# A gated delta-rule attention and mixture-of-experts kernel: the written order of one pipeline slot is replaced, and two more slots stand ahead of its loop

## The reference, cut to what matters

```python
def layer(x):                                  # x: 16 sequences of 512 tokens, 256 channels, f32
    x = x + layernorm(attn(layernorm(x)))
    return x + layernorm(experts(layernorm(x)))

def attn(x):                                   # H = 16 heads, DK = 64, DV = 128
    q, k, v = x @ w_q, x @ w_k, x @ w_v
    beta = 2 * sigmoid(x @ w_b)
    g = -exp(A_log) * softplus(x @ w_a + dt_bias)
    q, k, v = [silu(causal_conv(t, w, taps=4)) for t, w in ((q, conv_q), (k, conv_k), (v, conv_v))]
    q, k = q * rsqrt(sum(q * q) + 1e-6), k * rsqrt(sum(k * k) + 1e-6)     # per head
    for t in range(512):                       # per sequence and head, S is DK x DV
        S = S * exp(g[t])
        S = S + outer(k[t], (v[t] - k[t] @ S) * beta[t])
        o[t] = (q[t] * DK ** -0.5) @ S
    y = o * rsqrt(mean(o * o) + 1e-5) * norm_w * silu(x @ w_g)
    return y @ w_out                           # 2048 channels down to 256
```

## Time and profile before

| what | value |
|---|---|
| time, median of 3 runs | 4893.17 us (4889.53 to 4895.24) |
| the profiled execution: its time, and its span from first to last instruction | 4890.76 us, 4889.5 us |
| PE busy, PEld busy | 98%, 79% of the span |
| DVE, ACT, POOL busy | 86%, 71%, 64% of the span |
| delta phase on PE | first product of slot 0 at 124.66 us, last product at 4553.3 us |
| one ACT copy `b_Ue` or `b_Me`; one product of `c_y` on DVE (two in a step) | 374, 387 ns; 343 ns |
| mean granted TensorE clock | 0.991 of full speed |

### The profile page before, as it was taken

The page is one execution under the profiler, slowest core; times in us unless marked ns, Lnnn a source line. Parts: engine busy times, 40 slices in busy tenths (PEclk is TensorE's granted clock), DMA queues, the critical chain, the costliest instruction groups (busy, mean ns, idle before and its releaser), DMA issues. The chain is left out here.

```text
span 4889.5 us, 149087 instructions
## 1 busy us (share of the span) xinstructions
PE 4769.5 (98%) x44460; PEld 3838.5 (79%) x44460; DVE 4200.1 (86%) x9904; ACT 3471.9 (71%) x10299; POOL 3139.1 (64%) x4494
## 2 busy tenths in 40 slices
PE   7899999999999999999999999999999999999797
PEld 7688888888888888888888888888888888888565
DVE  3788888888888888888888888888888889998576
ACT  4677777777777777777777777777777777777443
POOL 3566666666666666666666666666666667777465
PEclk9999999999999999999999999999999999999899
DMA  5101111011110111011110111101010111111010
GB/s 195 50 34 41 42 41 44 33 39 37 43 41 31 40 39 41 32 39 44 37 41 32 39 41 39 38 33 47 34 39 32 39 45 45 60 45 45 17 40 31
DMA packets 123093, 210.98 MB, mean 43 GB/s; under 512 B 13154, under 2 KB 78836, under 8 KB 122868
## 3 DMA queue, kind: packets, MB, share of 16 engines
q1 hardware_dynamic: 121668, 207.24, 12.3%
q10 hardware_dynamic: 1200, 0.92, 0.1%
HBM read 188.32 MB, written 19.79 MB: 43 GB/s over the span
## 5 line engine op out<-in xcount | busy, mean ns | idle before, releaser
L741 DVE SCALAR_TENSOR_TENSOR cv<-ps_a,wqkv,cv 128x511 f32<-128x511 f32 (+2 forms) x1536 | 1132.2, 744 | 47.2 <-issue 15.4
L945 POOL TENSOR_TENSOR bm<-bat,mask 128x256 f16<-128x256 f32 x1536 | 1029.0, 692 | 0.1
L726 PE MATMUL ps_a<-xin,wqkv 128*128 128x512 f32 x2048 | 996.6, 609 | 2.4 <-issue 1.3
L940 POOL TENSOR_TENSOR tt<-bat,first 128x512 f16<-128x512 f32 x256 | 297.0, 1160 | 757.6 <-PE b L1027 757.5
L1006 DVE TENSOR_TENSOR tt<-tt,b 128x256 f16<-128x256 f16 x1536 | 638.8, 416 | 163.9 <-PE b L1001 147.3
L995 ACT ACTIVATE m<-b 128x256 f16<-128x256 f32 x1536 | 580.8, 387 | 216.3 <-PE b L990 207.4
L734 ACT ACTIVATE cv<-ps_a,wqkv 128x512 f32<-128x512 f32 x512 | 351.8, 687 | 505.4 <-PE ps_a L726 505.4
L1048 ACT CAST tt<-bu 128x256 f16<-128x256 f32 x1536 | 573.9, 374 | 102.4 <-PE bu L1043 84.4
L1180 PE MATMUL ps_a<-wout,yT 128*128 128x256 f32 x2048 | 557.4, 395 | 0.5 <-ACT yT L1174 0.5
L726 PEld LDWEIGHTS ps_a<-xin,wqkv 128*128 128x128 f32 x2048 | 350.3, 191 | 251.1 <-issue 251.0
L873 PE MATMUL ps_b<-wgate,xin 128*128 128x256 f32 x2048 | 502.0, 388 | 0.3 <-DVE ss L827 0.3
(11 more groups left out here) (230 smaller groups left out, 12046.8 us busy)
## 6 DMA issues: line engine op xcount, KB each, us to landing
xin<-xT_scratch SPq DMA_DIRECT2D x128, 512.0 KB, 3.3
grow<-g_scratch SPq DMA_DIRECT2D x128, 512.0 KB, 4.1
gam<-g_scratch SPq DMA_DIRECT2D x256, 96.0 KB, 2.8
n_x<-in_x SPq DMA_DIRECT2D x16, 512.0 KB, 3.7
xT_scratch<-n_xT SPq DMA_DIRECT2D x16, 512.0 KB, 2.6
out_y<-e_yo SPq DMA_DIRECT2D x16, 512.0 KB, 2.7
gate_tok<-in_x SPq DMA_DIRECT2D x56, 128.0 KB, 2.6
wqkv<-in_w_qkv SPq DMA_DIRECT2D x32, 128.0 KB, 2.9
```

The lines of the kernel that those rows point to most:

```text
L726: ins = pe.matmul(ps[:], wqkv[:, k, j * P:(j + 1) * P], xin[p][:, k, :], start=k == 0, stop=k == KT - 1)
L741: s.done(dve.scalar_tensor_tensor(y[:, r:], ps[:, 0:T - r], tap[:, j, TAPS - 1 - r:TAPS - r], y[:, r:], ALU.mult, ALU.add), f"a_tap{j}{r}")
L945: s.done(pool.tensor_tensor(half_of(bm[:, l, units(g), :], l, 1), half_of(bt[:, units(g), :], l, 1), half_of(c["mask"][:, l, :].unsqueeze( ...
```

## The change: another order of steps in a slot, and FIRST = 24

`SLOT_ORDER` is replaced. It holds the same 239 steps. Going around it once (the end joined to the start, since slots follow each other), TensorE changes 23 times from a step with f16 products to one with f32 products before, and 17 times after. The point at which a slot begins has also moved: 60 steps have crossed it, from the first part of the list to the last, with their lag one lower (12 steps from 1 to 0, 34 from 2 to 1, 14 from 3 to 2). All lags of the x_ steps are as they were. FIRST goes from 22 to 24, so the loop makes 46 passes instead of 47.

```diff
--- before.py
+++ after.py
 SLOT_ORDER = """
-    a_tap01.1 b_Ue51.3 c_R1.3 b_sq1.2 a_tap02.1 b_P1.3 b_V20.2 a_proj1.1 b_diag1.2 b_Ve20.2 c_Z1.3 b_R1.3 b_E0.1
...
+    a_silu1.1 c_acc0.3 c_sq1.3 c_KS2.3 c_m1.3 b_Ue01.2 b_Me40.2 b_V40.2 b_M11.2 c_R2.3 b_Me11.2 b_U40.2 b_kT.1
...
 """.split()
...
-FIRST = 22
+FIRST = 24
```

More of the change, by code:

```diff
@@ L52 @@
 SLOT_ORDER = """
-    a_tap01.1 b_Ue51.3 c_R1.3 b_sq1.2 a_tap02.1 b_P1.3 b_V20.2 a_proj1.1 b_diag1.2 b_Ve20.2 c_Z1.3 b_R1.3 b_E0.1
[L54 to L71, removed]
+    a_silu1.1 c_acc0.3 c_sq1.3 c_KS2.3 c_m1.3 b_Ue01.2 b_Me40.2 b_V40.2 b_M11.2 c_R2.3 b_Me11.2 b_U40.2 b_kT.1
+    c_p1.3 x_bn0.4 b_Ve40.2 c_Z2.3 b_Ue40.2 b_sq0.1 b_V11.2 c_y1.3 b_n0.1 b_M50.2 x_y0.5 b_U11.2 c_u2.3 c_yT1.3
@@ new lines @@
+    b_Ve11.2 b_Me50.2 b_kk0.1 b_V50.2 b_M21.2 x_x0.5 b_Ue11.2 b_ss.1 c_yTe1.3 b_Me21.2 b_U50.2 c_SU2.3 b_rc.1
+    c_O2.3 b_bm41.2 b_Ve50.2 b_w1.1 b_P0.2 b_V21.2 b_Ue50.2 b_ev00.1 b_E1.1 b_ev01.1 b_kw.1 c_S2.3 b_Ve21.2 b_U21.2
+    a_proj2.1 b_ktok.1 b_R0.2 c_sq2.3 c_m2.3 c_KS3.3 c_out1.3 c_p2.3 b_M31.2 x_bn1.4 c_y2.3 b_Ue21.2 a_cv2.1
+    a_tap21.1 x_y1.5 b_F0.2 c_yT2.3 b_diag0.1 b_vT0.2 b_t20.1 c_acc1.3 x_x1.5 a_tap22.1 c_R3.3 b_Me31.2 b_T0.2
+    a_tap23.1 b_V31.2 b_gam.1 b_hi0.1 a_tanh2.1 a_proj3.1 b_Ve31.2 c_Z3.3 b_Tq0.1 b_bm00.1 b_vtok0.2 a_cv3.1
@@ new lines @@
+    c_yTe2.3 b_U31.2 b_bm51.2 a_silu2.1 b_M41.2 b_Me41.2 b_Tf0.1 a_tap31.1 b_Ue31.2 b_g0.1 b_M00.1 c_u3.3 a_tap32.1
+    b_tg0.1 x_bn2.4 b_U41.2 b_V41.2 c_O3.3 b_Ue41.2 x_y2.5 a_tap33.1 c_out2.3 b_Me00.1 b_Ve41.2 b_U00.1 b_sg0.1
+    x_x2.5 b_M51.2 b_lo0.1 b_V00.1 a_tanh3.1 b_qT.1 a_silu3.1 c_Z0.2 c_acc2.3 c_sq3.3 b_bm10.1 b_Ve00.1 b_bm20.1
+    b_Me51.2 b_lo1.2 b_V51.2 b_kk1.1 b_Ve51.2 b_root.1 c_m3.3 c_p3.3 b_M10.1 b_Ue00.1 c_u0.2 b_sq1.1 b_U51.2
+    b_Me10.1 b_P1.2 c_y3.3 c_yT3.3 b_bm30.1 x_bn3.4 b_ev10.1 c_SU0.2 b_n1.1 x_y3.5 b_ev11.1 b_Ue51.2 c_yTe3.3
@@ new lines @@
+    b_V10.1 b_Ve10.1 b_U10.1 a_proj0 x_x3.5 b_bm40.1 c_O0.2 b_diag1.1 a_cv0 b_M20.1 c_S0.2 b_R1.2 c_out3.3 b_Ue10.1
+    b_sel x_mv.4 b_eps.1 b_Me20.1 a_tap01 c_sq0.2 x_ve.4 c_m0.2 b_gend.1 c_KS1.2 c_acc3.3 x_rs.4 c_p0.2 b_vT1.1
+    b_E0 b_V20.1 a_tap02 b_U20.1 b_F1.2 b_T1.2 c_R1.2 a_proj1 c_Z1.2 b_t21.1 b_bm01.1 b_bm11.1 b_kqs.1 b_Ue20.1
+    b_Ve20.1 b_M30.1 b_Tq1.1 a_tap03 c_y0.2 a_tanh0 b_bm21.1 b_vtok1.1 c_yT0.2 a_cv1 b_Me30.1 x_sh.4 a_silu0
+    b_Tf1.1 b_hi1.1 c_yTe0.2 b_g1.1 a_tap11 c_u1.2 a_tap12 b_V30.1 a_tap13 b_M01.1 b_Ve30.1 b_U30.1 b_tg1.1 c_SU1.2
@@ L72 @@
+    b_sg1.1 c_O1.2 b_M40.1 b_Me01.1 b_V01.1 b_Ue30.1 b_U01.1 c_out0.2 b_bm31.1 c_S1.2 b_bm50.1 b_Ve01.1 a_tanh1
 """.split()
```

## The result

The changed kernel takes 4938.22 us (median of 4 runs, 4937.54 to 4944.21) against 4893.77 for the kernel before in the same session: ratio 1.0091, 95% interval 1.0078 to 1.0104. It is slower, by 44 us. The forecast was 4889, the range ended at 4918.

What follows compares the result with a forecast made beforehand. TensorE's row of product steps was taken as the bound. Slot savings -72, start and end +2, output-weight waits +16, residual slots +46 and clock +4 sum to -4 us: median 4889 us, range 4866 to 4918.

Steps and rivals of the forecast that it cites:

- The saving per slot: In slots 3 to 128, fewer f16-to-f32 changes and a removed wait on TensorE save 0.57 us each, -72 us together.
- VectorE's short hand-overs: Products that need VectorE soon after c_KS2, c_Z2 and c_yT1, come late: 0.09 us per slot, bounds 0 and 0.3.
- Start and end: Slot 0 gets longer by some 8 us and the last two slots lose about as much: +2 us (-5 to +10).
- the wait for wo: TensorE waits 2 to 2.5 us at c_out0 for the output weights, once per pair of heads: seven times, +16 us.
- the chain at `x_x2`: In slots 117 to 128 GpSimd waits at x_x2 for x_y2, delaying TensorE up to c_yT3: 12 x 3.8 = +46 us.
- The clock: After the new waits TensorE's granted clock falls to half two or three times, 1.6 us each: +4 us.
- rival (a): Slower: the clock falls in nearly every residual slot and behind most output-weight waits, 18 falls, +29, 4914 us; chance 0.20.
- the two slots more ahead of the loop I put at nothing: Two more slots ahead of the loop cost 0, since slots ahead of it and inside it looked equally long.
- late next: The products expected to be late next, c_Z2 and c_yT1, wait for VectorE's c_R2 and c_y1: 0.09 us per slot.
- Rival (c): Slower: VectorE's many hand-overs to TensorE cost 0.3 us per slot instead of 0.09: +26, 4915 us; chance 0.11.
- (b): Faster: GpSimd's waits don't come; 4848 us without that at x_x2, 4873 without only the output-weight one; chance 0.17.
- (d): Slower: what fewer format changes save comes back elsewhere on TensorE, losing 0.46 us per slot: 4947 us; chance 0.05.

## Why the prediction was wrong, point by point

**The saving per slot was right, 0.57 us, in nearly every part.** By the steps' starts, 0.43 are format changes (forecast 0.46) and 0.14 the wait at `c_SU2` (forecast 0.15), which now starts 0.12 us behind `b_U50`:

```profile
642.22 0.28 PE L1042 MATMUL bu<-tt,m 128*128 128x64 f16 x4
642.34 0.69 PE L1101 MATMUL cs<-uu,ktok 128*128 128x128 f32 x4
```

Two small ones cancelled, so that the sum agrees to the hundredth is luck. One is `b_kk0`, which gave nothing: behind the transpose `c_yT1` it still starts 0.09 us late (0.34 instead of 0.25), so that gap belongs to `b_kk0` itself:

```profile
640.57 0.41 PE L1165 MATMUL co<-ident,yy 128*128 128x128 f32 x2
640.91 1.14 PE L908 MATMUL ps_a<-kq 64*128 64x256 f32 x8
```

The other is VectorE's short hand-overs, put at 0.09, which cost nothing ahead of the loop. Here are `b_kT`, `c_Z2` and the step behind them ahead of the loop, and then in the first slot of a pass:

```profile
639.28 0.63 PE L771 MATMUL ps_b<-ident,kq 128*128 128x128 f32 x4
639.75 0.63 PE L1085 MATMUL cs<-rr,tinv 128*128 128x128 f32 x4
640.22 0.28 PE L1000 MATMUL b<-m,tt 128*128 128x64 f16 x4
...
3166.64 0.64 PE L771 MATMUL ps_b<-ident,kq 128*128 128x128 f32 x4
3167.24 0.68 PE L1085 MATMUL cs<-rr,tinv 128*128 128x128 f32 x4
3167.76 0.28 PE L1000 MATMUL b<-m,tt 128*128 128x64 f16 x4
```

**Start and end, the wait for wo, the chain at `x_x2`: right in place and size** (+3, 19 and 41 us against +2, 16 and 46). One detail of the second: the first of the seven waits took 3.6 us and the others 2.6, the forecast was 2 to 2.5.

**The step that failed is the one called "The clock".** It put two or three falls at 1.6 us into the sum, 4 us. There were 19, one at every wait of 2.5 us and more, and 38 us: 15 lasted 3.4 us and four twice as long. That is rival (a), which the prediction priced rightly for 18 falls (+29, 4914 us) and gave 0.20. The one piece of evidence at hand, a stretch of 2.2 us idle and half clock behind it, spoke for (a). I set it aside with the thought that TensorE is dense around the new waits; no row bore that out, and the runs refute it. Where the waits were taken away, their falls went with them (4913.93 and 4872.82 us). Still, one row could not have settled it. In the experts phase of the changed kernel the same stretch of 2.2 us idle ends at 4638.4 us, and no fall follows; the next 46 us run at full clock:

```profile
4638.40:4684.00 45.60, 42.88 (x214) 30.64 (x215) 33.77 (x174) 21.73 (x44) 28.70 (x13) 1.00 0.06 24
```

**A second step failed: "the two slots more ahead of the loop I put at nothing", read as "a slot of the loop is as long as one ahead of it".** For FIRST itself it holds (4895.25 us). But the earlier trace rows showed only that the old order hid what the loop costs: there the products that came late had slack. In the new order a slot in the loop takes 0.09 us more, and 0.19 more again in the first slot of a pass. In the rows above `c_Z2` starts 0.13 us late in that slot and `b_V11` behind it 0.05; `b_M11` ahead of them is 0.08 late too. The jump stands just ahead of `c_acc0` and `c_R2` on VectorE, for which `c_Z2` waits, and with the jump elsewhere the 0.19 was gone. That is the "late next" place named in the prediction, with the price in the wrong slots. 17 us, and the run with all slots written out gives them back: 4841 to 4824.

Rivals (b) and (d) are refuted. Rival (c) named the right mechanism, VectorE's hand-overs, and took 0.21 us more per slot in all 126; measured were 0.185, in the 92 slots of the loop alone. With rival (a) for the clock and these 17 us the sum of the prediction would have been 4889 + 25 + 17 = 4931 us, and with the 19 falls as long as they were, 4940.

## What to carry to other kernels

A wait is priced with what follows it: here each idle stretch of 2.5 us on TensorE cost 4.2 to 5.7 (the stretch, and half of what lay behind it of the 3.4 or 6.8 us at half clock). When an order is made for the engine that bounds, look in it for the steps that are active only sometimes (residual steps, loads once per pair): they were not in what it was made for, and moving one step of each turned +0.9% into -1.0%. And when a kernel with a loop is edited, count the packets of instructions in the middle of the loop first: a shift of the code by a few instructions can cost more than any edit of the order did here.
